# Last attention of a fused eight-block kernel: keys brought by transfers, halves of exponentials added on GpSimd, sums one round later

## The reference, cut to what matters

```
def _L3_xattn_ref(query, key, value, Wq, bq, Wk, bk, Wv, bv, Wo, bo):
    H, dk = (16, 8)
    Q = (query @ Wq + bq).reshape(B, S, H, dk).transpose(0, 2, 1, 3)
    K = (key @ Wk + bk).reshape(B, S, H, dk).transpose(0, 2, 1, 3)
    V = (value @ Wv + bv).reshape(B, S, H, dk).transpose(0, 2, 1, 3)
    scores = jnp.einsum('bhqd,bhkd->bhqk', Q, K) / np.sqrt(dk)
    attn = jax.nn.softmax(scores, axis=-1)
    out = jnp.einsum('bhqk,bhkd->bhqd', attn, V)
    return out.transpose(0, 2, 1, 3).reshape(B, S, D) @ Wo + bo
...
    x = x + _L3_xattn_ref(_layernorm(x, axis=-1), ctx_1024, ctx_1024, L3_xattn_Wq, ...)
```

## Time and profile before

| | us |
|---|---|
| median of 3 runs | 980.13 (979.42 to 980.34) |
| the profiled execution | 979.69 |
| its span | 977.9 |
| TensorE busy | 846.0 (87%) |
| VectorE busy | 715.9 (73%) |
| ScalarE busy | 577.5 (59%) |
| GpSimd busy | 425.1 (43%) |

### The profile page before, as it was taken

The page is one execution under the profiler, slowest core; times in us unless marked ns, Lnnn a source line. Parts: engine busy times, 40 slices in busy tenths (PEclk is TensorE's granted clock), DMA queues, the critical chain, the costliest instruction groups (busy, mean ns, idle before and its releaser), DMA issues. The chain is left out here.

```text
span 977.9 us, 28764 instructions
## 1 busy us (share of the span) xinstructions
PE 846.0 (87%) x11577; PEld 636.2 (65%) x11577; DVE 715.9 (73%) x1700; ACT 577.5 (59%) x1328; POOL 425.1 (43%) x286
## 2 busy tenths in 40 slices
PE   5687998996579799799868999999999998978988
PEld 4555548885356568345646878878787877744567
DVE  5896878986543344899786858586776859889974
ACT  5564445775244453577686484756748484347874
POOL 4012206851456654597105343343516263619810
PEclk9698999999599999999988999999999999999999
DMA  7420004002511113000100000000100100000001
GB/s 226 128 88 1 1 1 188 2 2 56 206 42 47 42 41 107 1 2 2 55 1 2 29 3 29 4 29 3 29 20 12 31 2 3 3 2 1 2 2 44
DMA packets 27999, 36.36 MB, mean 37 GB/s; under 512 B 7163, under 2 KB 21692, under 8 KB 27102
## 3 DMA queue, kind: packets, MB, share of 16 engines
q1 hardware_dynamic: 22174, 28.11, 8.8%
q0 software_dynamic: 2496, 5.12, 1.9%
q10 hardware_dynamic: 3200, 1.31, 0.5%
HBM read 27.25 MB, written 7.27 MB: 35 GB/s over the span
## 5 line engine op out<-in xcount | busy, mean ns | idle before, releaser
L2218 DVE TENSOR_TENSOR soft_outs<-soft_expert_ps,soft_bias 128x512 f32<-128x512 f32 x128 | 87.3, 689 | 77.1 <-PE soft_expert_ps L1936 75.3
L1936 PE MATMUL soft_expert_ps<-soft_W,soft_slots 128*32 128x128 f32 x4096 | 126.2, 276 | 2.4 <-DVE soft_outs L2218 2.4
L1936 PEld LDWEIGHTS soft_expert_ps<-soft_W,soft_slots 128*32 128x32 f32 x4096 | 109.7, 111 | 21.5 <-issue 21.3
L2028 ACT ACTIVATE soft_slots<-soft_slot_ps 128x512 f32<-128x512 f32 x128 | 69.3, 596 | 65.1 <-PE soft_slot_ps L1922 65.1
L1039 POOL TENSOR_TENSOR l_prob<-l_prob,l_inv 128x1024 f32<-128x1024 f32 x48 | 91.2, 1900 | 32.6 <-DVE l_inv L1193 32.0
L2113 POOL TENSOR_TENSOR l_ring<-l_ring,soft_inv 128x1024 f32<-128x1024 f32 x15 | 35.1, 2368 | 104.7 <-DVE soft_inv L2211 54.6
L1883 PE MATMUL soft_slot_ps<-phi,xnT 128*128 128x256 f32 x256 | 67.7, 400 | 9.6 <-ACT soft_spread L2016 6.4
L1950 PE MATMUL soft_mix_ps<-soft_outs,soft_combT 128*32 128x128 f32 x2048 | 67.8, 273 | 2.1 <-DVE soft_acc L2234 2.1
L2113 POOL TENSOR_TENSOR soft_spread<-soft_spread,soft_inv 128x1024 f32<-128x1024 f32 x16 | 37.3, 2366 | 70.7 <-DVE soft_inv L2211 70.7
L1178 DVE TENSOR_REDUCE l_under<-l_score 128x16 f32<-128x1024 f32 x48 | 58.1, 1209 | 11.7 <-PE l_score L1262 6.3
L1883 PEld LDWEIGHTS soft_slot_ps<-phi,xnT 128*128 128x128 f32 x256 | 46.8, 197 | 20.7 <-ACT soft_spread L2016 7.2
(11 more groups left out here) (474 smaller groups left out, 2178.4 us busy)
## 6 DMA issues: line engine op xcount, KB each, us to landing
moe_w<-in_moe_W SPq DMA_DIRECT2D x2, 2048.0 KB, 10.0
soft_W<-in_soft_W SPq DMA_DIRECT2D x16, 256.0 KB, 2.6
kept<-early SPq DMA_DIRECT2D x1, 2048.0 KB, 6.3
l_keys<-in_moe_b SPq DMA_DIRECT2D x1, 2048.0 KB, 8.7
l_asked<-kept SPq DMA_DIRECT2D x1, 2048.0 KB, 13.1
x_tok<-in_x SPq DMA_DIRECT2D x4, 256.0 KB, 4.0
ctxT<-in_ctxT SPq DMA_DIRECT2D x1, 1024.0 KB, 7.6
moe_rows<-xn_tok SPq DMA_DIRECT2D x4, 256.0 KB, 3.5
```

The costliest lines, as they stand in the source:

```text
L1936: last = nc.tensor.matmul(expert_ps[c][32 * j:32 * j + 32, h, tt, :], slots[u % 3][:, h, tt, 128 * c + 32 * j:128 * c + 32 * j + 32], W[i ...
L2028: last = nc.scalar.activation(slots[u % 3][:, h], slot_ps[h][:], ACT.Copy)
L2218: nc.vector.tensor_tensor(outs[u % 3][:, c].rearrange("p h t d -> p (h t) d"), expert_ps[c][:].rearrange("p h t d -> p (h t) d"), bias[i % ...
```

## The change

In the last attention only (`kT` is given there alone):

- The keys of tiles 4 to 15 are no longer spread by GpSimd. Four more slots (`more`) are cleared once by GpSimd; the first four keep the zeros that `soft_moe` left. SyncE copies each head's eight rows of four tiles into its own columns: 16 transfers a batch, three batches. Batch 0 waits for the clearing, batch 1 for the scores of tile 3, batch 2 for those of tile 7. TensorE waits for a batch before tiles 4, 8 and 12.
- GpSimd adds the two halves of each head's exponentials (`add_halves`, 512 columns instead of 1024), and VectorE sums the result, of tile i-2 in round i and no longer of tile i-1. GpSimd's `share` too is that of tile i-2, behind the halves of tile i.
- The factor 8**-0.5 leaves `head_of` (now 0 and 1) for `take_early`, where ScalarE scales the keys of both attentions and the bias; that takes one activation of 128x1 more.

```diff
+                                         ACT.Identity, bias=(core.bk_scaled if c < G and not n else core.zero)[:, 0:1],
+                                         scale=8 ** -0.5 if c < G else 1.0).then_inc(early_taken, 1)
+
+            act.wait_ge(core.loaded["l3"], core.l3["loads"])
+            nc.scalar.activation(core.bk_scaled[:], core.l3["bk"][:], ACT.Copy, scale=8 ** -0.5).then_inc(early_taken, 1)
+            act.wait_ge(early_taken, 1)
...
@@ attend
+            half = [st.sb(f"half{p}", [128, 16, S // 2]) for p in range(2)]
+            more = st.sb("more", [128, 4, 8, 128])
+            first_keys = core.l3_ring[:].rearrange("p (t h s) -> p t h s", t=4, h=8)
...
+                for n, ring in enumerate((more[:], first_keys, more[:])):
+                    if n:
+                        sp.wait_ge(score_done, 4 * n)
+                    else:
+                        sp.wait_ge(more_zero, 1)
+                    own = kT[:, 512 * n + 512:512 * n + 1024].rearrange("p (t s) -> p t s", t=4)
+                    for r in range(16):
+                        rows = slice(8 * r, 8 * r + 8)
+                        sp.dma_start(ring[rows, :, r % 8, :], own[rows]).then_inc(keys_in[n], 16)
...
+            def add_halves(t):
+                pool.wait_ge(prob_done, t + 1)
+                if t >= 2:
+                    pool.wait_ge(total_done, t - 1)
+                nc.gpsimd.tensor_tensor(half[t % 2][:], prob[t % 4][:, :, 0:S // 2], prob[t % 4][:, :, S // 2:S],
+                                        ALU.add).then_inc(half_done, 1)
+
+            if halved:
+                nc.gpsimd.memset(more[:], 0.0).then_inc(more_zero, 1)
+                for i in range(T):
+                    add_halves(i)
+                    if there(i - 2):
+                        share(i - 2)
+                share(T - 2)
+                share(T - 1)
...
-                if t >= prepared:
+                if halved and t >= 4 and t % 4 == 0:
+                    pe.wait_ge(keys_in[t // 4 - 1], 256)
+                if not halved and t >= prepared:
                     pe.wait_ge(keys_done, t + 1 - prepared)
...
-                score(scores[t % 2], keys[t % 4], t).then_inc(score_done, 1)
+                score(scores[t % 2], keys[t % slots], t).then_inc(score_done, 1)
...
             def sum_up(t):
-                dve.wait_ge(prob_done, t + 1)
-                nc.vector.tensor_reduce(total[t % 2][:], prob[t % 4][:], AX.X, ALU.add).then_inc(total_done, 1)
+                if halved:
+                    dve.wait_ge(half_done, t + 1)
+                else:
+                    dve.wait_ge(prob_done, t + 1)
+                nc.vector.tensor_reduce(total[t % 2][:], half[t % 2][:] if halved else prob[t % 4][:], AX.X, ALU.add).then_inc(total_done, 1)
...
-                if there(i - 1):
-                    sum_up(i - 1)
-                    invert(i - 1)
+                for t in ((i - 2, i - 1) if i == T else (i - 2,) if i < T else ()) if halved else (i - 1,):
+                    if there(t):
+                        sum_up(t)
+                        invert(t)
```

More of the change, by code:

```diff
@@ L346, in _ @@
                 sp.dma_start(dst, src).then_inc(sem, 16)
-            sp.wait_ge(early_taken, 8)
+            sp.wait_ge(early_taken, 9)
             sp.dma_start(core.kept_dram, core.early[:]).then_inc(kept_out, 16)
@@ L430, in take_early @@
                     nc.scalar.activation(core.early[:, 512 * c:512 * c + 512], moved[2 + c % 2][:].rearrange("p k d -> p (k d)"),
-                                         ACT.Identity, bias=(w["bk"] if c < G else core.zero)[:, 0:1]).then_inc(early_taken, 1)
+                                         ACT.Identity, bias=(core.bk_scaled if c < G and not n else core.zero)[:, 0:1],
[3 more added lines that the diff above has]
+            act.wait_ge(early_taken, 1)
             take_early(0, core.l3)
@@ L496, in make_early @@
                     if n or c >= 2:
-                        pe.wait_ge(early_taken, 8 * n + c - 1)
+                        pe.wait_ge(early_taken, 8 * n + c)
                     bank = moved[2 + c % 2][:].rearrange("p k d -> p (k d)")
@@ L522, in _ @@
             pe.wait_ge(values_done, G)
-            pe.wait_ge(early_taken, 16)
+            pe.wait_ge(early_taken, 17)
             for g in range(G):
@@ L985, in attend @@
 def attend(nc, core, name, score, value, output, mix_scale, spread, keys, prepared, next_norm, sets=1, loads=(), read=None,
-           on_act=None, on_dve=None, beside=None, apart=False):
+           on_act=None, on_dve=None, beside=None, apart=False, kT=None):
     KEEP = 12
@@ L999, in attend @@
         total = [st.sb(f"total{p}", [128, 16]) for p in range(2)]
+        halved = kT is not None
+        if halved:
+            half = [st.sb(f"half{p}", [128, 16, S // 2]) for p in range(2)]
+            more = st.sb("more", [128, 4, 8, 128])
+            first_keys = core.l3_ring[:].rearrange("p (t h s) -> p t h s", t=4, h=8)
+            half_done, more_zero, keys_in = st.sem("half_done"), st.sem("more_zero"), [st.sem(f"keys_in{n}") for n in range(3)]
+            keys = list(keys) + [more[:, n].rearrange("p h s -> p (h s)") for n in range(4)]
+        slots = len(keys)
         inv = [st.sb(f"inv{p}", [128, 16]) for p in range(2)]
@@ L1040, in share @@
                                         ALU.mult).then_inc(share_done, 1)
[L1042 to L1048, removed]
-                if there(i - 1):
-                    share(i - 1)
+            def add_halves(t):
[4 more added lines that the diff above has]
+                                        ALU.add).then_inc(half_done, 1)
+            if halved:
+                nc.gpsimd.memset(more[:], 0.0).then_inc(more_zero, 1)
[6 more added lines that the diff above has]
+            else:
+                for t in range(prepared, 3):
+                    spread_keys(t)
+                for i in R:
+                    if there(i + 3) and i + 3 >= prepared:
+                        spread_keys(i + 3)
+                    if beside:
+                        beside(pool, i)
+                    if there(i - 1):
+                        share(i - 1)
         @block.tensor
@@ L1776, in head_attention @@
     attend(nc, core, name, score, lambda t, m: values[:, t, m], output, 1.0,
-           lambda out, t: spread_heads(nc, core, queries.kT, out, t), queries.ring, 1 if masked else 4, next_norm, **read)
+           lambda out, t: spread_heads(nc, core, queries.kT, out, t), queries.ring, 1 if masked else 4, next_norm, kT=None if masked else queries.kT, **read)
 def l2_attention(nc, core):
@@ L2503, in prepare @@
             core.l2 = w
-    core.head_of = sb("head_of", [128, 8])
+    core.head_of, core.bk_scaled = sb("head_of", [128, 8]), sb("bk_scaled", [128, 1])
     load("head_of", core.head_of[:], a["head_of"])
@@ L2579, in layout @@
     out["l3_bq"], out["l3_bk"] = v["L3_xattn_bq"][:, None], v["L3_xattn_bk"][:, None]
-    out["head_of"] = (np.arange(128)[:, None] // 8 % 8 == np.arange(8)).astype(np.float32) * np.float32(8 ** -0.5)
+    out["head_of"] = (np.arange(128)[:, None] // 8 % 8 == np.arange(8)).astype(np.float32)
     out["mask"] = v["mask_Bx1xSxS2_ik0"].reshape(T, 128, S).transpose(1, 0, 2)
```

## The result

| | before | after |
|---|---|---|
| median | 980.24 | 1029.47 |
| runs | 979.42 to 981.03, 4 | 1027.18 to 1031.26, 4 |
| the profiled execution | 979.69 | 1027.18 |
| its span | 977.9 | 1025.4 |

The medians are 49.2 us apart, a ratio of 1.0502. The ratio recorded with the result is 1.0485, with a 95% interval of 1.0458 to 1.0512, which is 47.5 us of 980.24. The sum in the prediction was made for 44; the time lies inside the stated range.

What follows compares the result with a forecast made beforehand. VectorE was taken as the bound, GpSimd close behind; after the change, a chain of waits. 979.69 + 39.2 (chain) + 5 (clock) = 1023.9, with the median 0.44 higher 1024.3 us; range 1015 to 1035.

Steps and rivals of the forecast that it cites:

- The sum in the prediction: Whole kernel: +39.2 us from the last attention's rounds at full clock, and +5 us from TensorE's slower clock.
- The step that decided: Last attention: exponentials, halves, share, turn and next exponentials wait on each other in turn, 6.56 us a round against 3.71.
- the sum: One round of the last attention: 1.67 + 0.08 + 1.16 + 1.90 + 0.08 + 1.67 = 6.56 us.
- Head and tail: Last attention: +2.70 us up to the exponentials of tile 3, +2.81 us from tile 15's to the turn of tile 13.
- The clock: TensorE in the last attention: idle 3.1 us a round lowers its clock, 5 of 14 turns slow, +5 us.
- My argument that a slow round brings the next ones back: TensorE in the last attention: steady work in a slow round restores the full clock, so 5 of 14 turns slow.
- The rival with the clock down in nearly every round: Last attention: 14 turns slow at 1.0 us each, total 1033.3 us; chance 0.12.
- What lay before the stage: Ahead of the last attention: key scale in ScalarE's copies and one 128x1 activation, zero, at most 0.3 us.
- The keys: Last attention, keys by transfer: zero cost, at most some 6 us once; 16 transfers issued in 7.5 us.
- its chain: Last attention: exponentials of one round wait on those of the round before through GpSimd and TensorE, 6.56 us a round.
- The sign that I named: In the changed profile, last attention: the score of tile 4 with no wait for a transfer.
- The gain: Last attention: shorter VectorE sums free 0.53 us a round, rounds from 3.71 to about 3.45 if nothing else ends later.

Runs made afterwards that it cites:

- e7: Changed kernel with 36 small matmuls added on TensorE before each turn of rounds 3 to 16; 1021.7 us by the ratio, 1.0423 to the kernel before.
- e1: Changed kernel with two GpSimd instructions exchanged: share of tile i-2 first, then halves of tile i; ratio 1.0049 to the kernel before.
- e2: e1 with VectorE also summing tile i-2 and taking its reciprocal before the largest of tile i; ratio 1.0014 to the kernel before.
- e6: Changed kernel with only the keys by transfer: no halves added, VectorE's sum and GpSimd's share as in the kernel before; ratio 1.0053 to that kernel.
- e5: e2 with the keys of tiles 4 and 5 spread by GpSimd, only tiles 6 and 7 in the first batch; ratio 0.9945 to the kernel before.

## Why the prediction was right

**The step that decided** was slack and order, not busy time, and every link was measured: 1.65 us of exponentials (1.67 in the sum), 0.08, halves and share 3.12 from the start of the one to the end of the other (3.06), 0.06 (0.08), and 1.66 from turn to exponentials (1.67). The halves took 1.26 us and not 1.16; the 0.10 was offset by an overlap of the two GpSimd instructions of 0.04 and by three other links that were 0.01 or 0.02 shorter, so the sum was right to 0.01 partly by luck.

**Head and tail.** +2.7 was worked out for the head and 3.4 measured, the first turn being a slow one (1.88 us). +2.8 was worked out to the turn of tile 13 and 2.8 measured. Behind it I expected nothing and 1.8 us came: the turn of tile 13 was slow (1.97) and that of tile 14 in part (1.62), together 1.4 us above 1.09 each.

**The clock.** That it would fall was right, how often was a guess. I took five slow turns at 1.0 us, from bounds of 0 and 14, and no row gave the five. The profiled execution has seven, those of tiles 0, 1, 2, 4, 7, 10 and 13, at 0.85 us each, as 7.42 - 6.57 shows: 6.0 and not 5. That this is near 5 is luck. My argument that a slow round brings the next ones back held in part: the first three turns were slow one after the other; from tile 4 on every slow one was followed by two fast ones. The rival with the clock down in nearly every round (the second in the prediction's list, which it calls the third) did not come: half of the 14 turns were slow. The Trainium skill (TensorE: Matmul & The Clock Gate, Part 1) has activity release the throttle; e7 agrees, with the clock at 1.00 once the idle time was filled.

**What lay before the stage** cost 1.4 us in this execution, where I had zero. As the experiments with the same code there began tile 0's exponentials anywhere between 874.88 and 879.55, I don't put it down to the change. The parts give 47.5 us between the two traced spans; the three other executions took 1.3 to 4.1 us more than the traced one and have no trace, so the last 1.7 us (49.2 between the medians, 47.5 between the spans) stay unexplained. A later start of the stage, which alone differs by up to 4.7 us among the experiments, would do it, and so would more slow turns; nothing decides between them.

**The keys.** That they would cost nothing was right for this kernel, but only because its chain was slower still. The sign that I named, scores of tile 4 with no wait for a transfer, did not come. I had 7.5 us for the issue of 16 transfers; it took 11.88, 0.74 each, and it began at 876.67 and not at 875.3:

```profile
876.67 11.88 SPq L1044 DMA_DIRECT2D l_more<-l_asked  x16
...
890.00 1.99 PE L1805 MATMUL l_score<-l_more,xn_tok 64*64 64x512 f32 x8 [1.44 <-DMA l_more<-l_asked]
...
893.99 1.97 PE L1108 MATMUL l_turned<-consts,l_prob 128*128 128x128 f32 x8 [0.99 <-POOL l_prob L1061]
```

The scores of tile 4 waited 1.44 us, and the turn behind them on TensorE still waited 0.99 for its share, so the end was not moved. As soon as the chain is gone (e1, e2, e6) the same wait is 4.2 to 6.8 us and costs most of that or all: the kernel with the keys alone (e6) has the rounds of before and a stage 5.2 us longer. The estimate of the issue came from transfers of another shape.

**The gain** that the change could have had was put at rounds of about 3.45 us; without the chain they are 3.37 (e2, e5), and TensorE is the bound (97% busy in e5), as read from its wait of 0.24 us.

## What to carry to other kernels

Before an instruction is moved behind a wait in an in-order engine's list, follow the ring from what it waits for to who waits for the instruction behind it, and back: the sum of that ring is a lower bound of the round, however idle the engines are. Work that is taken from a full engine gains only if its new place is off every such ring; here exchanging two instructions on GpSimd and moving two on VectorE turned 49 us of loss into 1.4, which can't be told from none, and two early tiles of keys turned that into a gain of 5.4, of which the trace shows 2.9 in the stage. A prefetch that "has time" should be counted by its issue, transfer by transfer, and against the fast version of the kernel, not the slow one that hides it.

## What the runs showed of the hardware

- Issuing a transfer of eight partitions with four rows of 512 bytes each, SBUF to SBUF, took SyncE 0.74 us (11.88 for 16), and just as long with two such rows (e5, 11.88 for 16), where loads of 256 KB from DRAM in the earlier trace rows took 0.42. Between these two sizes, 16 KB and 8 KB, the number of transfers sets the time of the issue and their size does not.
- GpSimd's addition of 128x512 with operands of 32-element runs took 1.26 us, against 1.16 of the 65x512 one with whole rows, and 0.24 to 0.25 for 128x16.
- In the changed kernel, where TensorE was idle about 3.1 us in a round of 6.57, the clock was at 1.2 GHz for the turns of the first three tiles and, from tile 4 on, for every third. In e7, with 1.0 us idle before the turn, it stayed at 2.4 GHz for the turns of tiles 2 to 12, and for tile 13's behind 1.95 us. The lower clock made the turn 0.88 us longer and the round 0.85.
